# Eight attention heads over a product-key table: from three and a half heads multiplied in full and four and a half gathered, to four and four

## The reference

```python
h = tok_ref(x, ...)                       # pooled attention, 16 pixels to one token
h = h + attn_ref(layernorm(h), ...)       # two selective scans, one in each direction
h = h + ffn_ref(layernorm(h), ...)        # attention over a product-key table
```

```python
scores, idx = top_k(sim, 16)                          # sim: two sides x 64 keys
score = scores[0][..., :, None] + scores[1][..., None, :]
final_scores, pk_idx = top_k(score.reshape(..., 256), 16)
kv_scores = softmax(final_scores)
k = einsum('bnhk,bnhkd->bnhd', kv_scores, keys_table[ind])
v = einsum('bnhk,bnhkd->bnhd', kv_scores, values_table[ind])
out = causal_attention(q, k, v) @ Wo
```

## Time and profile before

| | |
|---|---|
| runs | 13362.06, 13356.86, 13354.56 us (median 13356.86) |
| the profiled execution | 13354.71 us, span 13352.6 us |
| mean granted TensorE clock | 0.933 of full |
| busy: PE, PEld, DVE, ACT, POOL | 88%, 70%, 78%, 55%, 77% |
| GpSimd's indirect DMAs | 9216 |
| matmuls on 56 slots' `o` and `z` | 3584 each |

### The profile page before, as it was taken

How to read it: one execution, slowest core, us unless ns; L and a number is a source line. 1 busy time by engine, 2 the same in 40 slices (tenths; PEclk the granted TensorE clock), 3 DMA queues, 4 the chain that set the end, 5 groups by cost and what they waited for, 6 DMA issues and landing times.

```text
span 13352.6 us, 262103 instructions
## 1 busy us (share of the span) xinstructions
PE 11719.0 (88%) x71396; PEld 9286.1 (70%) x71396; DVE 10428.1 (78%) x39940; ACT 7363.4 (55%) x17030; POOL 10215.8 (77%) x9220
## 2 busy tenths in 40 slices
PE   3888888988989889989889888898888888898988
PEld 3677677776777767777767677776677677776776
DVE  7878778778778787787777877877878878778772
ACT  2555555555555555555555555555555555555554
POOL 1777777777777777777777777777777777777776
PEclk6999999999999999999999999999999999999999
DMA  2555555555555555555555555555555555555554
GB/s 73 160 145 153 157 145 154 154 144 159 145 151 158 144 154 153 147 156 148 149 159 146 151 159 143 155 154 146 157 143 153 159 145 153 158 142 157 152 140 120
DMA packets 1668219, 1983.98 MB, mean 149 GB/s; under 512 B 532846, under 2 KB 1134062, under 8 KB 1666286
## 3 DMA queue, kind: packets, MB, share of 16 engines
q1 hardware_dynamic: 1371566, 1359.71, 35.8%
q0 software_dynamic: 294912, 604.57, 17.5%
HBM read 1898.00 MB, written 65.01 MB: 147 GB/s over the span
## 4 chain that ended last, share of the span: by engine, by line
PE 38%; DVE 26%; POOL 18%; issue 11%; DMA 4%; ACT 2%; SPq 0%; DVEq 0%; POOLq 0%; ACTq 0%
POOL gath L801 18%; PE bank L991 9%; PE bank L1032 6%; PE bank L873 4%; PE bank L1019 3%; DVE apart L1701 3%; PE bank L1006 3%; DVE row_f L1704 3%; DMA gath<-in_table_dram,rowsT 2%; DVE decay L1576 2%; PE bank L954 2%; DVE onehot L1803 2%; PE bank L977 2%; PE bank L1050 1%; DMA moving<-keyspace 1%
## 5 line engine op out<-in xcount | busy, mean ns | idle before, releaser
L801 POOL DMA_INDIRECT gath<-in_table_dram,rowsT x9216 | 10215.6, 1108 | 3105.9 <-issue 2673.7
L1256 ACT ACTIVATE weight<-bank 128x512 f32<-128x512 f32 x3584 | 2139.3, 597 | 4415.0 <-PE bank L1006 4383.9
L991 PE MATMUL bank<-weight,rowtab 128*128 128x256 f32 x12288 | 3373.8, 399 | 0.0
L1032 PEld LDWEIGHTS bank<-spread,gath 128*128 128x128 f32 x18432 | 2519.7, 201 | 727.8 <-DMA gath<-in_table_dram,rowsT 607.6
L1032 PE MATMUL bank<-spread,gath 128*128 128x96 f32 x18432 | 2524.3, 282 | 519.0 <-DMA gath<-in_table_dram,rowsT 518.8
L991 PEld LDWEIGHTS bank<-weight,rowtab 128*128 128x128 f32 x12288 | 2460.7, 202 | 620.3 <-issue 102.2
L1249 ACT ACTIVATE bank<-bank,seventeen 128x512 f32<-128x512 f32 x3584 | 2370.6, 661 | 13.3 <-PE bank L1006 10.2
L1019 PE MATMUL bank<-moving,pick_b 96*128 96x512 bf16 x3584 | 1457.5, 407 | 304.7 <-ACT bank L1249 226.5
L1006 PE MATMUL bank<-moving,pick_b 96*128 96x512 bf16 x3584 | 1435.0, 400 | 71.1 <-DMA moving<-keyspace 70.6
L1568 DVE TENSOR_TENSOR_SCAN decay<-decay,wide 128x1024 f32<-128x1024 f32 x512 | 1169.3, 2285 | 26.4
L1836 DVE SCALAR_TENSOR_TENSOR acc<-bank,rrow,acc 128x64 f32<-128x64 f32 x1024 | 240.5, 276 | 839.3 <-PE bank L1006 797.2
(11 more groups left out here) (268 smaller groups left out, 18929.9 us busy)
## 6 DMA issues: line engine op xcount, KB each, us to landing
rowtab<-in_tableD_dram SPq DMA_DIRECT2D x2048, 256.0 KB
wide<-states SPq DMA_DIRECT2D x512, 512.0 KB
moving<-keyspace SPq DMA_DIRECT2D x3072, 64.0 KB
gath<-in_table_dram,rowsT POOLq DMA_INDIRECT x9216
pix<-in_x_dram SPq DMA_DIRECT2D x504, 256.0 KB
moving<-keyspace SPq DMA_DIRECT2D x3072, 32.0 KB
keyspace<-split SPq DMA_DIRECT2D x192, 256.0 KB, 2.1
moving<-keyhalf SPq DMA_DIRECT2D x512, 64.0 KB
```

Of the source, the lines that this page charges most:

```text
L801: pool.indirect_dma_start(out=gath[:, u % RING, j, :], out_offset=None, in_=table, in_offset=bass.IndirectOffsetOnAxis(ap=rowsT[k][:, col: ...
L991: mm(dense_ps[:, 0:TOK], rowtab[:, r, s % 2 * 2 + half, :], weight[s % 2][:, half * TOK:(half + 1) * TOK], start=(s % 16 == 0 and half == ...
L1032: mm(sums_ps[:, col:col + STREAM], gath[:, u % RING, j, :], flat[:, col:col + STREAM], start=True, stop=True)
L1256: ins = af(weight[s % 2][:], zd_ps[s % 2][:], ACT.Exp, scale=-1.0)
```

## The change

Head 3 becomes fully dense. `DENSE` goes from 3 to 4, so there are 64 slots (16 for each of four heads), 32 gather parts (128 indirect DMAs per image), and 8 table slots' worth of half products become 16 of full ones. The table tiles loaded per image stay 32. The ring of gather parts goes from 6 to 4. The four orders are stretched to 64 rows: `g` parts stand in every second row, and most pieces stand a few rows later, in the same sequence. Two `R` pieces (R8, R9), `X5`, `selh`, `wb4`, `l2` and `k4` disappear, with the code for the half head.

```diff
-DENSE = 3
+DENSE = 4
-HU = DU + TILES
+HU = DU
-SLOTS = 16 * DENSE + 8
+SLOTS = 16 * DENSE
-PARTS = (GH * SPAN - SPAN // 2) // PART
-RING = 6
+PARTS = GH * SPAN // PART
+RING = 4
-ORDER = (1, 2, 3, 4, 0)
...
 PE_ORDER = """
-0 z55-1 a5.6-1 o0+0 d54-1 a6.0-1
-1 z0+0 d55-1 o1+0 S.A3+0 F.g+1
-2 z1+0 o2+0 d0+0 g0.0+0 a6.3-1
+0 z63-1 o0+0 d62-1
+1 z0+0 d63-1 o1+0 g0.0+0 a5.6-1 S.A3+0 F.g+1
+2 z1+0 o2+0 d0+0 a6.0-1
...
-4 z3+0 o4+0 d2+0 F.kv0+2 S.E3+0
+5 z4+0 o5+0 d3+0 g0.2+0 F.kv0+2 S.E3+0
...
-34 z33+0 o34+0 d32+0 F.xd+2 F.dt+2
-35 z34+0 a2.6+0 o35+0 d33+0 g2.6+0 a3.0+0
-36 z35+0 o36+0 d34+0 g2.7+0 S.E0+1
-37 z36+0 o37+0 d35+0 a3.3+0
+39 z38+0 o39+0 d37+0 g2.3+0 a2.5+0 F.xd+2 F.dt+2
+40 z39+0 o40+0 d38+0
+41 z40+0 o41+0 d39+0 g2.4+0 a2.6+0 S.E0+1
+42 z41+0 o42+0 d40+0 a3.0+0
+43 z42+0 o43+0 d41+0 g2.5+0
+44 z43+0 o44+0 d42+0 a3.3+0
...
-48 z47+0 o48+0 d46+0 g3.7+0 F.S0+2
-49 z48+0 d47+0 a4.6+0 o49+0 a5.0+0 F.S1+2
...
-55 z54+0 o55+0 d53+0 S.E2+1 F.y+2
+55 z54+0 o55+0 d53+0 g3.3+0 a4.5+0 F.S0+2
+56 z55+0 o56+0 d54+0 F.S1+2
+57 z56+0 o57+0 d55+0 g3.4+0 a4.6+0 F.S2+2
+58 z57+0 o58+0 d56+0 a5.0+0 F.S3+2 S.A2+1
...
+63 z62+0 o63+0 d61+0 g3.7+0 a5.5+0 S.E2+1 F.y+2
 DVE_ORDER = """
-0 a5.6-1 F.y+1 F.ps+2
-1 S.R9+0 S.e6+0
-2 S.R0+0 F.g+1
-3 S.re3+0 a6.3-1 S.e7+0
-4 S.lo3+0 S.R1+0 S.wb2+0 S.wb3+0 F.h2+1
+0 F.y+1 F.ps+2
+1 S.R7+0 S.e6+0
+2 a5.6-1 F.g+1
+3 S.re3+0 S.e7+0
+5 a6.3-1 S.lo3+0 S.wb2+0 S.wb3+0 F.h2+1
...
-17 a0.3+0 F.q0+2
+19 F.q0+2
...
-29 S.wx+1 S.sel+1 S.A0+1 S.G0+1
+33 S.wx+1 S.sel+1 S.A0+1 S.G0+1
...
-38 a3.3+0 S.wg+1 S.e3+1 F.B0+2
+43 S.wg+1 S.e3+1 F.B0+2
+45 a3.3+0 F.sf0+2
...
-47 a4.5+0 S.X5+1 S.wb0+1 F.C0+2
+54 S.wb0+1 F.C0+2
...
-51 S.selh+1 F.C3+2
+58 a4.6+0 F.C3+2
...
-54 S.lo2+1 a5.5+0 S.R8+1 S.e5+1
+62 S.lo2+1 S.R6+1 S.e5+1
 SP_ORDER = """
-35 bc+2 m38+0
+40 bc+2 t22+0 m43+0
...
     def product_part(b, s, half):
-        if h < DENSE:
-            mm(dense_ps[:, 0:TOK], rowtab[:, r, s % 2 * 2 + half, :],
-               weight[s % 2][:, half * TOK:(half + 1) * TOK], ...)
-        else:
-            for q in (2 * half, 2 * half + 1):
-                mm(dense_ps[:, 0:P], rowtab[:, r, q, :], weight[s % 2][:, q * P:(q + 1) * P], ...)
+        mm(dense_ps[:, 0:TOK], rowtab[:, r, s % 2 * 2 + half, :],
+           weight[s % 2][:, half * TOK:(half + 1) * TOK], ...)
...
-                    for j in range(PART):
-                        col = ORDER[g] * SPAN + u % 8 * PART + j
+                    for j in range(PART):
+                        col = g * SPAN + u % 8 * PART + j
```

More of the change, by code:

```diff
@@ L252 @@
-54 S.lo2+1 a5.5+0 S.R8+1 S.e5+1
-55 S.wb1+1
+0 F.y+1 F.ps+2
+1 S.R7+0 S.e6+0
+2 a5.6-1 F.g+1
+3 S.re3+0 S.e7+0
+4
+5 a6.3-1 S.lo3+0 S.wb2+0 S.wb3+0 F.h2+1
+6 S.n0+1 F.rf+2
+7 a6.5-1 S.n1+1
+8
+9
+10 a6.6-1 S.T0+1 S.T1+1
+11 S.T2+1 S.T3+1
+12
+13 a7.3-1 S.T4+1 S.T5+1
+14 S.T6+1
+15 a7.5-1 S.T7+1 S.T8+1 F.var+2
+16 S.T9+1 S.T10+1
+17 S.T11+1 F.nw0+2
+18 a7.6-1 S.T12+1 S.T13+1
+19 F.q0+2
+20
+21 a0.3+0 F.q1+2
+22 S.T14+1 F.q2+2
+23 a0.5+0 S.T15+1 S.T16+1
+24 F.pv0+2
+25 F.pv1+2
+26 a0.6+0 S.T17+1 S.T18+1 F.pv2+2
@@ new lines @@
+27 S.T19+1 S.cp+1 S.i+1
+28
+29 a1.3+0 S.pr0+1 S.L0+1 S.L1+1
+30 S.L2+1 S.L3+1 F.h1+2
+31 a1.5+0 S.wd+1 S.pr1+1
+32 F.nw1+2
+33 S.wx+1 S.sel+1 S.A0+1 S.G0+1
+34 a1.6+0
+35 S.A1+1 S.G1+1 F.uz0+2
+36
+37 a2.3+0 S.re0+1 S.e0+1
+38 S.G2+1 F.uz1+2
+39 a2.5+0 S.e1+1 S.lo0+1
+40 S.G3+1 S.re1+1
+41 F.dl+2
+42 a2.6+0 S.G4+1 S.e2+1 S.lo1+1
+43 S.wg+1 S.e3+1 F.B0+2
+44
+45 a3.3+0 F.sf0+2
+46 S.wh+1 F.sb0+2
+47 a3.5+0 F.B1+2 F.sf1+2
+48 F.sb1+2
+49 F.B2+2 F.sf2+2
+50 a3.6+0 S.R0+1 F.sb2+2
+51 F.B3+2 F.sf3+2
@@ L254 @@
+52
+53 a4.3+0 S.R1+1 F.sb3+2
+54 S.wb0+1 F.C0+2
+55 a4.5+0 F.C1+2
+56 S.R2+1 S.R3+1
+57 S.A2+1 S.A3+1 F.C2+2
+58 a4.6+0 F.C3+2
+59 S.R4+1 S.R5+1
+60
+61 a5.3+0 S.re2+1 S.e4+1
+62 S.lo2+1 S.R6+1 S.e5+1
+63 a5.5+0 S.wb1+1
 """
@@ L296 @@
 39 m42+0
-40 st0+1 t22+0 m43+0
-41 st1+1 m44+0
-42 lq0+2 t23+0 m45+0
+40 bc+2 t22+0 m43+0
+41 m44+0
+42 t23+0 m45+0
 43 m46+0
[L301 to L312, removed]
+44 t24+0 m47+0
+45 m48+0
+46 st0+1 t25+0 m49+0
+47 st1+1 m50+0
+48 lq0+2 t26+0 m51+0
+49 m52+0
+50 lq1+2 t27+0 m53+0
+51 m54+0
+52 t28+0 m55+0
+53 lq2+2 m56+0
+54 t29+0 m57+0
+55 lq3+2 m58+0
+56 t30+0 m59+0
+57 m60+0
+58 t31+0 m61+0
+59 m62+0
+60 t0+1 m63+0
+61 m0+1
+62 t1+1 m1+1
+63 m2+1
 """
@@ L635, in table_tile @@
         def table_tile(s):
-            return s // 2 if s < 16 * DENSE else s - 8 * DENSE
+            return s // 2
         def part_name(u):
@@ L1695, in second @@
                         done("pr1")
-                    for other in ("sel", "selh"):
-                        if other in mark:
-                            after(mark[other])
+                    if "sel" in mark:
+                        done("sel")
                     if "R" in mark:
@@ L1725, in second @@
                     mark["i"] = step(v.tensor_copy(idx_b[:], best_i[:, :, 0:HU, :]))
-                if name in ("sel", "selh"):
-                    lo, hi = (0, DU) if name == "sel" else (DU, HU)
-                    for other in ("L" if name == "sel" else "X",):
-                        if other in mark:
-                            after(mark[other])
+                if name == "sel":
+                    lo, hi = 0, DU
+                    if "L" in mark:
+                        done("L")
                     if "R" in mark:
@@ L1788, in second @@
                     side, t = n // 2, n % 2
-                    for other in ("i", "sel", "selh"):
+                    for other in ("i", "sel"):
                         if other in mark:
```

413 lines of the change are left out of this document (169 added, 244 removed).

## The result

The changed kernel takes 14332.99 us (median of 4 runs, 14292.67 to 14336.26), the kernel before beside it 13355.71: a ratio of 1.0724 [1.0705, 1.0744]. It is 7.2% slower, where 3.1% faster was forecast. The profiled execution is the fastest of the four (14292.67 us, span 14290.8).

The account below looks back on a forecast made before the run. GpSimd's gathers were taken to bound the kernel at 204.1 us per image. Stages A to D of 81, 47, 35.5 and 35.3 led to a 197.5 us period; -422 us, plus 10 for fill and drain, made 12,940 us; range 12,600 to 13,400.

Parts of the forecast that it names:

- stage A: First attention score of number 3 to end of `E3`'s onehots (scans, row numbers): 93.9 us to fall to 81.
- GpSimd leaves the path: With 16 of 144 gathers gone, GpSimd needs 184 us per image, stops being the bound and is slack by over 10.
- PE's work +6.8: Eight added slots cost PE 10.3 us per image, four removed gather parts save 3.5: 6.8 us more at full clock.
- DVE -6: R8 and R9 (3.9 us) and small pieces (about 2 us) go: VectorE does 6 us less per image, nearly all in stage A.
- ACT's round +2.2: Five more rows with only `z`, `o`, `d`, where PE waits 0.44 us each for ScalarE: 2.2 us per image.
- `moving` +1.2: Less cover for the load behind `bc`: PE waits 1.2 us more per image, between 0 and 2.5.
- Ring of four 0: Gather parts in stage A come as fast as PE asks, 6.2 us each: the smaller ring costs 0, up to 3 us.
- every other loss stays: Rival: only 8.4 us of gather waits leave PE, so +1.8 us per image, 13,480 us; chance 0.15.
- the clock comes back: Rival: A and C regain full clock as gather waits go, period 191.7 us, 12,570 us; chance 0.14.

Follow-up runs that it names:

- e4: Changed kernel with F and S pieces back at their old rows up to row 38, scan stage stretched from 18 to 26 rows: 13804.02 us.
- e1: Kernel before with two of each gather part's four indirect DMAs left out, PE reading the others twice: 13054.27 us.
- e13: e4 with all eight `a.6` ahead of their row's `o`, and `acc` one row earlier and first: 13090.96 us, 0.9804 of the kernel before.
- e14: Changed kernel with ScalarE's Relu on 256 of a slot's 512 columns: 14140.79 us.
- e15: Changed kernel with only e13's `a.6` and `acc` edit, on a slow chip: 15465.26 us, where the kernel before took 17400.44.
- e3: Changed kernel with seven gather parts of a period moved one row up into nearly empty rows: 14471.68 us, 1.0831 of the kernel before.
- e2: Changed kernel with two of each gather part's four indirect DMAs left out, PE reading the others twice: 14080.42 us.
- e6: The kernel of e13, run on a slow chip: 15400.42 us.
- e8: The kernel of e13, run on another slow chip than e6: 15261.98 us.
- e5: The kernel of e14, run on a slow chip: 15469.78 us.
- e9: The kernel of e14, run on a slow chip: 15383.74 us.
- e12: Changed kernel unchanged, run again beside e13 and e14 on one chip: 14410.18 us.

## Why the prediction was wrong

**The step that failed** is the reading of the change as a pure stretch. I priced how many rows hold nothing but a slot and how much cover `moving` has, and took the rest as the same pieces "in the same sequence". They are not. `a.6` had moved behind `o`, `d` and `g`, and `acc` behind a piece of F or S. The sum has no term for that, and the waits for `acc` were in the rows I had read the earlier trace rows. Put back on top of e4, it is worth 713 us, 11.1 us a period; the miss is 14.7 + 6.6 = 21.3 (the period grew by 14.7 us and was to shrink by 6.6), and e4's places have 8.3 more of it. Together that is 19.4 of the 21.3. What `acc` is worth in the changed kernel without e4's places is not shown.

**The second step that failed** is in the sum of stage A: that PE's waits for gathers go, that VectorE's idles go with them, and that the new rows lie under VectorE. In e1, with the old order, 411 of the 519 us came back at `decay`, 6.4 us a period. In neither kernel whose stages were read is A at 81 us: it is 98.4 and 87.7 after and 89.7 in e13, with VectorE idle for 24.1, 13.5 and 14.7 us of it.

Point by point, per image:

- *GpSimd leaves the path*: right. PE's wait for gathers went from 519 us to none, POOL's for PE from 172 to 2157 (over 800 was foretold). e1 bounds the worth of that at 4.7 us a period, and stage A of my sum had 7.5 for VectorE's two idles that were to go with it and with the place of a5.6.
- *PE's work +6.8*: PE is busy for 672.6 / 64 = 10.5 us more. The 3.7 us beyond I put down to half-clock time, which I had left as it was: L1000's kind takes 403 ns, 399 before and 389 in e13. The remainder itself was not measured.
- *DVE -6*: (10428.1 - 10043.9) / 64 = 6.0. Right, and it did not shorten A: VectorE's idle took its place.
- *ACT's round +2.2*: the term was mis-sized. The wait went from 226.5 to 606.1 us, +5.9. I took 0.44 us for five rows; in four images it is now 49 waits of 0.78 us instead of 28 of 0.44. e14 shows that this wait is on the path.
- *`moving` +1.2*: +2.2 (209.7 against 70.6 us), within the bound of 2.5.
- *Ring of four 0*: right; no product waits for a gather, and 57 short waits stand in e4.
- *Stage A 81*: wrong, 98 and 88. Of VectorE's 14.4 us of idle there the two of the earlier trace rows were to give 7.5; it is 24 and 13 instead. Over the whole run its idle at the first maximum grew from 917 to 1984 us.
- *`acc`*: no term, +5.3 (565.9 against 228.0 us). *`decay`*: no term, +3.2 (270.1 against 68.1). e1 shows where it can come from: the order before, which also has `F.S0` one row behind VectorE's `F.C0`, waits 479.1 us there once gathers no longer hold PE. e4, which has it two rows behind and more of F and S under the scans, takes nearly all of it back; which of the two does it was not separated.

Idle thus adds up to -8.1 + 5.9 + 5.3 + 3.2 + 2.2 - 2.5 (`onehot`) - 1.1 (`kvd`) and some smaller ones; the page says +265.6 / 64 = +4.15. With 10.5 of busy time that is the 14.7 us which a period has lost.

*The rival "every other loss stays"* had the right side, and the point from which it decides: VectorE's idle in A staying at 11 us (it is 24 and 13). Its price of +1.8 us took the losses as constant; the period lost 13 us more than that.

*The rival "the clock comes back"* named what the runs then showed to be large, for another cause. In e1, without gather waits, busy and idle fell by the same 150 us. In e13 idle fell by 271 us against e4 and busy by 431. The Trainium skill ("TensorE: Matmul & The Clock Gate", A second HAM failure mode: psum-queue depth-cycling) says that in one kernel frequent short idles between groups of matmuls made the clock swing. These traces don't bear that out as the main cause here: e13 has 983 waits for the Relu, 0.67 us in the mean, at a clock of 0.964, and the kernel after has 184 waits for `acc`, 3.1 us in the mean, at 0.921. Here the clock came back when the longer ones went; that the one made the other is argued from these counts and not tested by itself.

What stays open: how `a.6` and `acc` back alone do in the changed kernel on a chip of the first kind (e15 met the other); why e3's clock is lower; what fewer gathers give e2 beside the keys; and why the kernel before loses 4,000 us on the second kind of chip and those with 64 slots about 2,200 (e13's kernel).

## What to carry to other kernels

When an order written by hand is stretched, compare each pair of engines that hand work back and forth, and not only the rows: which piece now stands ahead of the consumer on each side. Take the ones that PE waits for in the profile of before, and look them up in the new order first. A wait that is taken away may have covered the next one: here 411 of 519 us came back at the next place where VectorE was late (e1). Price an idle of PE by what it does to the clock too: here an edit gave 713 us where the wait that it was for is 639 us shorter in the profile, half of which stood up again elsewhere. And where a verdict is to hold on many chips, run both kernels on more than one.

## What the runs showed of the hardware that was not expected

- The same program (e13, e6, e8) took 13,091 us on one chip and 15,262 and 15,400 on two others, and the kernel before 13,356 and 17,170 to 17,400. For the kernel of e14, the changed one with the shorter Relu, the verdict turns round: 1.059 of the kernel before on the one, 0.890 and 0.896 on the others (e5, e9). In the traces, ScalarE, VectorE and PE of the slow ones idle without a releaser that the profile knows, VectorE up to 13.5 us at a time.
- Half as many gathers made a kernel 1.8% faster that never waited for one (e2); 132 of the 212 us were PE's busy time, at a clock of 0.932 for 0.921; two traces of one kernel (after, e12) differ by 110 us in that.
- Seven gather parts a period moved by one row left PE's idle as it was (1888 us for 1899 and 1907), and busy time was 111 to 221 us longer, at a granted clock of 0.899 for 0.914 and 0.921 (e3 against e12 and after).
